# Planning the weight loads and row copies behind the second attention as steps of SyncE, and norming FFN outputs tile by tile

## What is computed

```
def _layer(x, wqkv, qs, ksc, wo, lg, lb, w1, b1, w2, b2):
    q, k, v = split(shift_token(x) @ wqkv)        # 8 heads of 64
    q, k = l2norm(q) * qs, l2norm(k) * ksc        # then rotary with scales
    x = x + local_attention(q, k, v) @ wo         # windows of 128, the one before and this
    h = shift_token(x)                            # right half of the columns from the row above
    h = (h - mean) / sqrt(var + 1e-5) * lg + lb
    a, g = split(h @ w1 + b1)                     # 682 each
    return x + (a * gelu(g)) @ w2 + b2
...
return layernorm(x + two_layers(x))
```

## Time and profile before

| | us |
|---|---|
| median of three runs | 2961.43 |
| the profiled execution | 2961.68 |
| its span, first to last instruction | 2959.4 |
| TensorE busy | 2835.6 (96%) |
| VectorE busy | 2176.4 (74%) |
| ScalarE busy | 1653.3 (56%) |
| GpSimd busy | 1048.7 (35%) |

### The profile page before, as it was taken

One profiled execution on the slowest core, in us unless ns is written; L12 is line 12 of the kernel. 1 busy time (PEld: TensorE's weight loads), 2 busy tenths in 40 slices (PEclk: granted clock), 3 DMA queues, 4 the chain that ended last, 5 costly groups with the idle time before them and its releaser, 6 DMA issues.

```text
span 2959.4 us, 52471 instructions
## 1 busy us (share of the span) xinstructions
PE 2835.6 (96%) x20384; PEld 1908.3 (64%) x20384; DVE 2176.4 (74%) x5057; ACT 1653.3 (56%) x3488; POOL 1048.7 (35%) x1208
## 2 busy tenths in 40 slices
PE   8998999999999999999997899999999899999997
PEld 7777877333333333333336788888878788888886
DVE  7885545788788778868846777777867577788784
ACT  3222332665565666556664576666666666666662
POOL 5333432033113212511314344434454444444441
PEclk9999999999999999999997999999999999999998
DMA  2000010321321322132203000000010100000001
GB/s 78 23 9 22 8 22 3 43 24 17 35 26 12 39 24 26 17 46 26 37 1 98 5 5 5 4 5 5 11 37 14 31 21 4 18 5 12 12 11 59
DMA packets 46284, 66.64 MB, mean 23 GB/s; under 512 B 9662, under 2 KB 34260, under 8 KB 46036
## 3 DMA queue, kind: packets, MB, share of 16 engines
q1 hardware_dynamic: 46036, 63.29, 12.0%
HBM read 24.99 MB, written 8.39 MB: 11 GB/s over the span
## 4 chain that ended last, share of the span: by engine, by line
PE 75%; DVE 11%; DMA 6%; POOL 3%; ACT 2%; issue 1%; SPq 1%; POOLq 0%; DVEq 0%; ACTq 0%
PE ps L1394 17%; PE pw L218 13%; PE ps L218 11%; PE pw L1381 10%; PE ps L1180 5%; DMA e_hs<-x 4%; PE pw L1180 4%; PE ps L1554 4%; PE pw L1467 2%; PE pw L1505 2%; PE pw L1330 1%; PE pw L1487 1%; DVE stat L1837 1%; DVE e_ot L2132 1%; PE ps L1467 1%
## 5 line engine op out<-in xcount | busy, mean ns | idle before, releaser
L1682 ACT ACTIVATE c_p<-pw 128x512 f32<-128x512 f32 x1024 | 562.3, 595 | 341.2 <-PE ps L1364 183.5
L1394 PE MATMUL ps<-c_p,c_vals 128*64 128x512 f32 x2048 | 547.4, 618 | 2.7 <-ACT c_p L1682 1.4
L1968 DVE TENSOR_REDUCE c_mx<-ps 128x1 f32<-128x512 f32 x694 | 462.7, 683 | 114.3 <-PE ps L1364 106.7
L1381 PE MATMUL pw<-c_qst,c_kst 50*128 50x512 f32 x1024 | 385.1, 449 | 9.4 <-DMA c_qst<-c_mr 9.0
L1381 PEld LDWEIGHTS pw<-c_qst,c_kst 50*128 50x128 f32 x1024 | 154.5, 185 | 368.2 <-ACT c_p L1682 272.1
L1364 PE MATMUL ps<-c_kst,c_qst 48*128 48x512 f32 x694 | 289.5, 452 | 4.6 <-DMA c_kst<-shared 3.5
L1736 ACT ACTIVATE e_sm<-e_sm,e_mx 128x256 f32<-128x256 f32 x512 | 253.9, 498 | 62.0 <-DVE e_mx L2113 61.9
L1968 DVE TENSOR_REDUCE c_mx<-pw 128x1 f32<-128x512 f32 x330 | 225.5, 683 | 47.3 <-PE pw L1364 43.8
L2233 POOL TENSOR_SCALAR stat<-stat 128x1 f32<-128x1 f32 (+1 forms) x138 | 32.1, 233 | 623.4 <-DVE stat L1840 352.0
L1394 PEld LDWEIGHTS ps<-c_p,c_vals 128*64 128x64 f32 x2048 | 104.2, 135 | 181.2 <-issue 162.1
L218 PE MATMUL pw<-shared,e_xb 128*128 128x512 f32 x792 | 216.9, 412 | 2.2 <-DVE e_xb L2062 1.5
(11 more groups left out here) (316 smaller groups left out, 6441.0 us busy)
## 6 DMA issues: line engine op xcount, KB each, us to landing
c_kst<-shared SPq DMA_DIRECT2D x192, 64.0 KB
c_qst<-shared SPq DMA_DIRECT2D x64, 128.0 KB
x<-in_L_attn_x SPq DMA_DIRECT2D x8, 512.0 KB, 3.8
c_qst<-shared SPq DMA_DIRECT2D x64, 64.0 KB
keep<-x SPq DMA_DIRECT2D x8, 512.0 KB, 4.5
e_raw<-keep SPq DMA_DIRECT2D x8, 512.0 KB, 3.5
out<-x SPq DMA_DIRECT2D x8, 512.0 KB, 5.9
e_hs<-x SPq DMA_DIRECT2D x64, 63.5 KB
```

Of the source, the lines that this page charges most:

```text
L1381: e.matmul(bank_of("c_s", n, sh, kt, h), c_kst[i][p0:p0 + 50, sh // 2, 128 * kt:128 * kt + 128], c_qst[i][p0:p0 + 50, sh // 2, 512 * h:512 ...
L1394: ins = e.matmul(pv[64 * h:64 * h + 64, :], c_v[:, kt, 33 * hd:33 * hd + 64], p[:, 512 * h:512 * h + 512], start=kt == 0, stop=kt == 7, sk ...
L1682: e.activation(c_p[slot["c_p", (n, sh, kt)]][:, 512 * h:512 * h + 512], bank_of("c_s", n, sh, kt, h), ACT.Exp, scale=0.5).then_inc(SC, 1)
L1968: e.tensor_reduce(c_mx[m % 2][:, qt, h:h + 1], bank_of("c_max", n, sh, qt, h), AX.X, ALU.max).then_inc(VE, 1)
```

## The change

Four things change, all in stage d, and no instruction of the arithmetic differs but for how many tiles one step takes.

1. A weight piece is three steps: `w_in` on SyncE (0.7 us for each transfer, landed 2.2 us later), `w_out` on ScalarE after the landing, `w_out` on GpSimd after that, which alone gives the buffer back.
2. The copy of shifted rows is a step of SyncE (1.3 us, landed 1.8 us later) with a due time of its own. VectorE's row of zeros is written down with the residual, and waits for the buffer.
3. `f_add` is four steps, one for each tile, each waiting for its own copy of rows; in layer 1 each tile has its own `n_st` on VectorE and GpSimd and its own `n_nm`. Their sums have 18 places in the columns of `stat` that single-tile norms leave free.
4. The numbers that steer the planner: `PERIOD`, `LATE`, `EPS`, `LAG` and most of `DUE`.

```
-PERIOD, LATE, SPREAD, EPS, LAG = 21, 63.6, 1.36, 0.13, 0.05
+PERIOD, LATE, SPREAD, EPS, LAG = 20.72, 65.97, 1.36, 0.1, 0.08
-        "pe f_down": 1.53, "dve f_add": 1.75, ...
-        ... "dve n_st f": 2.4, "pool n_st f": 1.4, "dve n_nm f": 1.9,
+        "pe f_down": 1.53, "dve f_add": 0.44, ...
+        ... "dve n_st f": 0.6, "pool n_st f": 0.8, "dve n_nm f": 0.42,
+        ... "sp d_hs": 1.3,
-DUE = {"pe d_qk": 13.7, "act d_qk": 3.7, "dve d_rope": 12.8, "pe d_turn": 5.6, "act d_turn": -19.7, "dve d_ss": 43.6,
-       "pool d_r": 16.5, "dve d_add": -21.6, "dve d_scale": 2.1, "pe d_v": 15.5, "act d_v": 22.3, "pe d_sim0": 22.8,
...
-       "act d_o": 30.9, "dve d_ol": 37.9, "pe d_wo": 15.7, "dve d_wo": 38.1, "dve n_st": 49.9, "pool n_st": 33.8,
-       "dve n_nm": 43.9, "d_x": -1.4}
+DUE = {"pe d_qk": 14.3, "act d_qk": -3.5, "dve d_rope": 9.6, "pe d_turn": 7, "act d_turn": -34, "dve d_ss": 43.9,
+       "pool d_r": 37.5, "dve d_add": -15.6, "dve d_scale": -17, "pe d_v": 14.8, "act d_v": 17.8, "pe d_sim0": 33.1,
...
+       "act d_o": 29.5, "dve d_ol": 40.3, "pe d_wo": 32.9, "dve d_wo": 20.5, "dve n_st": 49.8, "pool n_st": 36.1,
+       "dve n_nm": 41.4, "d_x": -17}
...
             def fetch(due, key, hi, lo, src, after):
+                i = (key,)
+
                 def begin(t):
-                    weight_in(raws, "raw_d", d_raw, key, hi, lo, src, None, ("act", "pool"), after)
-
-                def split(t):
-                    weight_out(raws, key)
-                    raws.idle.sort(key=room_at)
-                    over_at["pool", "w_out", (key,)] = engine_at["pool"] = max(engine_at["pool"], t + LAG) + TOOK["pool w_out"]
-                    settle([("pool", "w_out", (key,))])
-
-                raw_free = dict(takes=[(room_of_raws, "raw", *key)])
-                op(due, "sp", "w_in", (key,), after=after, place=begin, **raw_free)
-                op(due, "act", "w_out", (key,), after=[("sp", "w_in", key)], gives=[(room_of_raws, "raw", *key)], place=split)
-
-            room_of_raws = Ring(range(2))
+                    r = slot["w_in", i]
+                    weight(key, d_raw[r], hi, lo, src, None, ("act", "pool"), after)
+                    P.land(f"raw_d{r}", len(src), "w_in", key)
+                    P.add("w_in", key)
+                    over_at["dma", "w_in", i] = t + 2.2
+                    settle([("dma", "w_in", i)])
+
+                op(due, "sp", "w_in", i, after=after, takes=[(raws, "w_in", key)], place=begin, took=0.7 * len(src))
+                op(due, "act", "w_out", i, after=[("dma", "w_in", key)])
+                op(due, "pool", "w_out", i, after=[("act", "w_out", key)], gives=[(raws, "w_in", key)])
...
                 def residual(t):
                     P.add("d_wo", l, win, dve=1)
+                    if win % 8 == 0:
+                        P.add("d_hz", l, win, dve=1)
+
+                def moved(t):
                     P.land(f"hs{slot['d_hs', (l, win)]}", 2 if win % 8 else 1, "d_hs", l, win)
-                    P.add("d_hs", l, win, **({} if win % 8 else {"dve": 1}))
-                    over_at["dma", "d_hs", n] = t + 2.6
+                    P.add("d_hs", l, win)
+                    over_at["dma", "d_hs", n] = t + 1.8
                     settle([("dma", "d_hs", n)])
...
+                op(due + DUE["dve d_wo"] - 9, "sp", "d_hs", n, after=[("dve", "d_wo", *n)], place=moved)
...
-                put(len(chain), "dve", "f_add", n_of=4, after=[("pe", "f_down", *n, 5)] + hs_read + [("pool", "f_r3", bk)] * l,
-                    gives=[(acc, "f_acc", *n, k) for k in range(2)])
+                for j in range(4):
+                    tile = 4 * bk + j
+                    put(len(chain), "dve", "f_add", j, after=[("pe", "f_down", *n, 5), ("dma", "d_hs", l, tile if tile % 8 == 7 else tile + 1)] +
+                        [("pool", "f_r3", bk)] * l + [("dve", "f_add", *n, j - 1)] * (j > 0),
+                        gives=[(acc, "f_acc", *n, j // 2)] * (j % 2))
+                    if l:
+                        i, t = ("f", tile), PERIOD * (4 * b + 4) + LATE + pace * 19 + j
+                        op(t, "dve", "n_st", i, 2, [("dve", "f_add", *n, j)] + ([("dve", "n_nm", "f", tile - 8)] if tile > 7 else []))
+                        op(t, "pool", "n_st", i, 2, [("dve", "n_st", *i)])
+                        op(t, "dve", "n_nm", i, 1, [("pool", "n_st", *i)])
...
-                    op(t, "dve", "n_st", ("f", bk), 8, [("dve", "f_add", 1, bk)])
-                    op(t, "pool", "n_st", ("f", bk), 2, [("dve", "n_st", "f", bk)])
-                    op(t, "dve", "n_nm", ("f", bk), 4, [("pool", "n_st", "f", bk)])
```

More of the change, by code:

```diff
@@ L898, in window @@
                     last = [("pe", "d_v", *ago(1))] if g else []
-                    rows = ([("dve", "f_add", 0, win // 4)] if l else [("dve", "n_nm", "c", t) for t in range(win, win + 4)] if win < 24
+                    rows = ([("dve", "f_add", 0, win // 4, j) for j in range(4)] if l else [("dve", "n_nm", "c", t) for t in range(win, win + 4)] if win < 24
                             else [("dve", "n_nm", "c4", (win - 24) // 4)])
@@ L1155, in x_by @@
         def x_by(l, win):
-            bk, tile = divmod(win, 4)[0], win
             if l:
-                return dve("f_add", l - 1, bk)
-            return dve("n_nm", "c", tile) if tile < 24 else dve("n_nm", "c4", (tile - 24) // 4)
+                return dve("f_add", l - 1, *divmod(win, 4))
+            return dve("n_nm", "c", win) if win < 24 else dve("n_nm", "c4", (win - 24) // 4)
         def norm_tiles(stage, i):
-            return [i[0]] if stage in ("a", "c") else [24 + 4 * i[0] + t for t in range(4)] if stage == "c4" else [
+            return [i[0]] if stage in ("a", "c", "f") else [24 + 4 * i[0] + t for t in range(4)] if stage == "c4" else [
                 4 * i[0] + t for t in range(4)]
@@ L1171, in build @@
         for kind, i, marks in P.steps:
-            if kind == "n_st" and "dve" in marks:
+            if kind == "n_st" and "dve" in marks and i[0] != "f":
                 norm_slot[i] = len(norm_slot) % 6
         def st_of(*i):
+            if i[0] == "f":
+                return stat[:, i[1] // 3 % 6, 1 + i[1] % 3:, :]
             return stat[:, norm_slot[i], :, :]
@@ L2138, in d_wo_, with d_hz @@
                 e.tensor_tensor(x[:, win, :], x[:, win, :], bank_of("d_wo", l, win)[:, 0:256], ALU.add).then_inc(VE, 1)
-            def d_hs_(l, win):
-                if win % 8 == 0:
-                    e.memset(d_hs[slot["d_hs", (l, win)]][0:1, :], 0.0).then_inc(VE, 1)
+            def d_hz(l, win):
+                for s in freed("d_hs", l, win):
+                    w.wait_ge(*s)
+                e.memset(d_hs[slot["d_hs", (l, win)]][0:1, :], 0.0).then_inc(VE, 1)
             def f_x(l, bk, k):
@@ L2179, in f_hp, with f_add @@
                     e.memset(raw32(hp[32:64, 1, :]), 0.0).then_inc(VE, 1)
-            def f_add(l, bk):
+            def f_add(l, bk, j):
+                tile = 4 * bk + j
                 w.wait_ge(*pe("f_down", l, bk, 5))
@@ L2184, in f_add @@
                     w.wait_ge(*pool("f_r3", bk))
-                for j in range(4):
-                    tile = 4 * bk + j
-                    w.wait_ge(*dma("d_hs", l, tile if tile % 8 == 7 else tile + 1))
-                    e.tensor_tensor(x[:, tile, :], x[:, tile, :],
-                                    bank_of("f_acc", l, bk, j // 2)[:, 256 * (j % 2):256 * (j % 2) + 256],
-                                    ALU.add).then_inc(VE, 1)
+                w.wait_ge(*dma("d_hs", l, tile if tile % 8 == 7 else tile + 1))
+                e.tensor_tensor(x[:, tile, :], x[:, tile, :],
+                                bank_of("f_acc", l, bk, j // 2)[:, 256 * (j % 2):256 * (j % 2) + 256], ALU.add).then_inc(VE, 1)
             play("dve", dict(b_begin=b_begin, c_begin=c_begin, d_begin=d_begin, ident=ident_, w_out=w_out, n_st=n_st, n_nm=n_nm, a_x=a_x,
@@ L2229, in n_st @@
             def n_st(stage, *i):
-                st, n = st_of(stage, *i), 1 if stage in ("a", "c", "d") else 4
+                st, n = st_of(stage, *i), 1 if stage in ("a", "c", "d", "f") else 4
                 w.wait_ge(*dve("ident"))
@@ L2491, in store @@
             def store(i):
-                w.wait_ge(*dve("n_nm", "f", i))
+                for t in range(4 * i, 4 * i + 4):
+                    w.wait_ge(*dve("n_nm", "f", t))
                 e.dma_start(xout[:, 4 * i:4 * i + 4, :], x[:, 4 * i:4 * i + 4, :]).then_inc(sems[f"x{i}"], 16)
```

12 lines of the change are left out of this document (6 added, 6 removed), and 6 rows, old and new, of the table DUE.

## The result

The changed kernel takes 2969.49 us (median of six runs, 2967.42 to 2972.96) against 2957.44 us (2954.41 to 2961.51) of the kernel before: ratio 1.0040, 95% interval 1.0027 to 1.0053. It is slower by 0.4%, where 2938 us and a gain were forecast. Its profiled execution took 2968.73 us, with a span of 2966.3.

A forecast was written before the change was run, and what follows sets the result against it. TensorE was taken as the bound, busy 457.7 of 460 us in mid layer 0, with losses elsewhere in stage d. Terms -14 - 12 + 2 = -24 took 2961.7 to 2938 us; own range 2922 to 2951, eight in ten 2906 to 2970.

The forecast's parts named there:

- New due times: Layer 0: taken as 0; at most 2.3 us idle to win, loss bounded at 22 us.
- The slower rival: Layer 0 takes on layer 1's pattern, statistics waiting for copies ahead of the rotary: +22, around 2976 us; chance 0.15.
- Weight pieces, -14: Head and change of layers: shorter waits for weight pieces win 10 us idle and 4 us of clock.
- Copies, 0: VectorE stands some 0.5 us less before statistics, 33 us in 62 cases, covered by TensorE's other work.
- Tiles, -12: Layer 1: one tile ahead of a residual takes 8 us off waits for k, plus 4 us of clock.
- Tail, +2: End of stage d: about one FFN product more left when the windows end, +2 us.
- The ports: Layer 1: further GpSimd pairs hold up VectorE through the shared-port lock, 19 us, 2957 us; chance 0.08.

The follow-up runs named there:

- e2: Kernel before with the new PERIOD, LATE, EPS, LAG and due times alone, old steps; 2996.32 us, ratio 1.0134.
- e24: e19 with the new PERIOD, LATE, EPS and LAG and the old due times; 2966.95 us, ratio 1.0032.
- e25: e19 with the new due times and the old PERIOD, LATE, EPS and LAG; 2975.76 us, ratio 1.0057.
- e3n: Changed kernel with the weight pieces planned the old way; 2968.06 us, ratio 1.0038.
- e3: Kernel before with the weight pieces as three steps, nothing else; 2960.61 us, ratio 1.0013.
- e7: Kernel before with weight pieces and row copies as steps, no single tiles, old numbers; 2960.94 us, ratio 1.0012.
- e5: Kernel before with only the copies of shifted rows as steps of SyncE; 2940.81 us, ratio 0.9939.
- e11: e4 with the second to fourth add of a block due at once, norms still by tile; 2953.19 us, ratio 0.9987.
- e14: Changed kernel without the single tiles: weight steps, copy steps and the new numbers; 2975.35 us, ratio 1.0063.
- e17: e5 with statistics and norms by tile in layer 1, the four adds one step, old numbers; 2942.46 us, ratio 0.995.
- e19: Kernel before with copies as steps, norms by tile with adds together, weight steps for layer 1 only, old numbers; 2939.17 us, ratio 0.9945.
- e22: Kernel before with copies as steps and weight steps for layer 1 only, no tile steps, old numbers; 2937.76 us, ratio 0.9935.
- e8: Kernel before with the row copy counted as landed after 5.6 us instead of 2.6; 2978.61 us, ratio 1.0069.
- e4: Kernel before with only the adds, statistics and norms of FFN outputs tile by tile; 2991.15 us, ratio 1.0111.

## Why the prediction was wrong, point by point

- **New due times: the step that failed.** I wrote "I take 0, because the same work at the same bound fills the list so long as anything is ready". e2 shows 18 us lost in layer 0 with the new numbers alone, e24 and e25 that each half of them takes the pace away. Two things were wrong. TensorE's busy time is not the same for every order of the same matmuls (1.6 us more a block), and the new list had 1.2 us more of short idle waits a block on the chip. The bound that I had set beside it, 3.1 us for each of 7 blocks or 22 us, held: 18 us over five blocks. The slower rival named the place and nearly the price, and its 2972 us is 2.5 us off. That is in part luck: it had +22 in layer 0, -14 for the weight steps and +2 in the tail, where the runs have +18.0, -8.4 in the change of layers and -3.1 in layer 1. Its mechanism, statistics that wait for a copy and get ahead of the rotary, is not borne out: VectorE stood before copies for as long in the middle of layer 0 as before (39.3 and 39.6 us).
- **Weight pieces, -14.** ScalarE's waits fell as said (26.6 to 10.0), and the single waits over 3 us left the change of layers. But e2 and e3n have neither of these waits with the old weight steps, so the 8.4 us won there come with the numbers; the steps' own gain there, 12.5 us, shows at the old numbers only (e3). For the head I took the same cure, and at the old numbers it was a loss of 9 us (e3) to 25 (e7 against e5). Net: nothing (e3, and e3n against after). The step that failed is that a wait taken off ScalarE is taken off the path. In e3's head two others took its place: a piece held up behind a copy of rows (6.3 us of TensorE) and VectorE standing before a copy, ahead of the maxima (5.5 us).
- **Copies, 0.** The stand of VectorE before the statistics fell by 13 us in e5 (130.0 to 116.8) and by 3 in after, not by 33; that it is covered holds in the middle of layer 0, and not in the head of e3 and e7. What I missed is the other end of the step: taken out of the residual, the copy no longer holds up the loads behind it in SyncE's list. I noted that the copies "are now planned between the loads" and gave it no price. e5 gives -17 us, of which the issue rows and the waits behind them account for a part in the head. In the changed kernel none of it is seen: its head ends at 1776.6, as before.
- **Tiles, -12.** Mis-sized: e11 gives -4 to -5, and by which mechanism is open, since the slow adds beside GpSimd went with it. Unsized was that four steps can come apart, +34 us at the old numbers. At the new ones they stay together in the steady blocks, and the tiles are worth some -6 (after against e14), most of it in layer 1 (585.1 against 591.4 us).
- **Tail, +2.** The rest behind the last block's add is 9.5 us, before 9.9: nothing.
- **The ports.** This rival fell, with the opposite sign: what it called a cost of more GpSimd instructions is a cost of one kind of them, and the tile steps took it away in e11, e17 and e19.

VectorE's norms of FFN tiles and rotary adds in layer 1 (2360 to 2900), in e22 without the tile steps, then in e19 with them (total, then mean ns of one):

```profile
L1877 DVE TENSOR_SCALAR x<-x,stat 128x256 f32<-128x256 f32 x24 | 16.3, 739 | 0.0
...
L2114 DVE TENSOR_TENSOR e_tq<-e_tq 128x512 f32<-128x512 f32 x24 | 22.8, 949 | 0.0
```

```profile
L1883 DVE TENSOR_SCALAR x<-x,stat 128x256 f32<-128x256 f32 x26 | 9.7, 392 | 1.7 <-POOL stat L2263 1.7
...
L2120 DVE TENSOR_TENSOR e_tq<-e_tq 128x512 f32<-128x512 f32 x24 | 16.3, 681 | 0.0
```

The same norm takes 392 ns instead of 739, the same rotary add 681 instead of 949, though GpSimd has more instructions. The means hide two groups. VectorE and GpSimd of e22, a slow add and four norms, each with what ran beside it, then a fast add (the first line of each pair is GpSimd's):

```profile
2440.32 1.60 POOL L2381 TENSOR_TENSOR e_hp<-e_hf,e_hp 124x512 fp32r<-124x512 f32 x1
2440.71 1.76 DVE L2114 TENSOR_TENSOR e_tq<-e_tq 128x512 f32<-128x512 f32 x1
```

```profile
2447.95 1.29 POOL L2381 TENSOR_TENSOR e_hp<-e_hf,e_hp 124x512 fp32r<-124x512 f32 x1
2447.00 2.72 DVE L1877 TENSOR_SCALAR x<-x,stat 128x256 f32<-128x256 f32 x4
```

```profile
2398.55 2.92 POOL L2360 TENSOR_TENSOR e_ss<-e_ss,half 128x16 f32<-128x16 f32 x1
2400.33 0.68 DVE L2114 TENSOR_TENSOR e_tq<-e_tq 128x512 f32<-128x512 f32 x1
```

In e22 all six adds of 1.75 us run beside GpSimd's subtraction over 512 columns, and the six norms of 1.45 us as well; six more norms that run into it take 0.70, and the other norms 0.40. Beside the powers and the short instructions that follow them every add takes 0.68 us, and in e19, where no norm meets a subtraction, the norms take 0.36 to 0.41 us beside the short powers of `stat`. The lock of the Trainium skill (SBUF — State Buffer, "SBUF: two separate sides"), exclusive and held for the whole instruction, fits the subtraction. It does not fit the power: held for the whole of its 2.9 us it would have held up the add that started 1.8 us into it, and six adds in the stretch start so and take 0.68 us. The profile's times of GpSimd are rough. The further pairs of short instructions, which I had priced at 0.8 us each, cost these norms nothing that shows; what counts is when the subtractions of `e_hp` fall.

What stays open: how much of the 1.6 us a block is waits too short to show as idle time, why only the old numbers reach 80.0 us, and what made the first block behind the head 86.7 us long.

## What to carry to other kernels

A list made by a greedy planner and due times fitted to it are one thing: here a truer estimate, a finer step or new numbers alone cost 0.7 to 1.3% (e8, e4, e2), so change one step at a time at the old numbers, and read the pace of a steady block before the total. When a step is split whose parts hold a shared buffer between them, keep the parts together; here that was worth 38 us. Split a mean by what ran beside each instance, before a price is put on a count of instructions. A step that one engine starts for another has two ends: ask also what is queued behind it on the queue that plays it.

## What the runs showed of the hardware

- The order of the same matmuls at full clock changes TensorE's busy time: 79.7 and 81.3 us for 690 and 691 of them (before and after). Waits of up to 0.16 us behind a 128x512 matmul are in it.
- Two halves of scores (16 matmuls of 64x128 each) in a row take 1.99 us, each alone 1.09, and the 128x512 matmul ahead of a run of scores takes 0.33 us to the next start instead of 0.23.
- Beside GpSimd's `tensor_tensor` on 124x512 a 128x512 add of VectorE took 1.75 us instead of 0.68 and a 128x256 norm 1.45 instead of 0.40 (e22). Beside GpSimd's power on 128x16, 2.9 us long, the add took 0.68.
- A copy of 63.5 KB from SBUF to SBUF, one partition lower, took 5.0 us from its start to the engine that waited for it.
